# One PSUM bank per head for the first scores of an attention decoder

## The reference

```
# windowed cross attention to the context, 16 heads of 16 features, |i - j| <= 64
scores = where(local, q @ k.T / 4, -inf);  p = softmax(scores);  ctx = p @ v
# cell of six nodes, each an attention of 8 heads of 32 features
q = ew0 * (n_q @ We_q + b);  k = ...;  v = ...
o = softmax((q Wq)(k Wk).T / sqrt(32)) @ (v Wv) @ Wo;   node = act_w * o + q
# cross attention of layer 1, 16 heads of 16 features, padded keys masked
p = softmax(where(mask, ln(q) @ ln(k).T / 4, -inf));  ctx = p @ v
```

## Time and profile before

| | us |
|---|---|
| median of three runs | 3567.08 (3566.13 to 3568.82) |
| the profiled execution | 3568.07 |
| its span in the trace | 3566.3 |
| PE busy | 3242.3 (91% of the span) |
| DVE busy | 2329.9 (65%) |
| ACT busy | 1695.1 (48%) |
| POOL busy | 1019.1 (29%) |

### The profile page before, as it was taken

One profiled execution on the slowest core, in us unless ns is written; L12 is line 12 of the kernel. 1 busy time (PEld: TensorE's weight loads), 2 busy tenths in 40 slices (PEclk: granted clock), 3 DMA queues, 4 the chain that ended last, 5 costly groups with the idle time before them and its releaser, 6 DMA issues.

```text
span 3566.3 us, 77500 instructions
## 1 busy us (share of the span) xinstructions
PE 3242.3 (91%) x31372; PEld 2395.2 (67%) x31372; DVE 2329.9 (65%) x4137; ACT 1695.1 (48%) x3472; POOL 1019.1 (29%) x795
## 2 busy tenths in 40 slices
PE   7899999998999999899999999999899999999876
PEld 6777767676766667676666766667676666766644
DVE  6675658667676766767577675766767676464533
ACT  1244454544545455444635445354454545554532
POOL 7872006042331413333041332304233141000000
PEclk8999999999999999999999999999999999999986
DMA  6210011010101101010100101101010110100000
GB/s 207 89 45 31 19 29 39 29 40 19 46 19 40 31 23 46 16 41 26 37 28 25 43 19 37 31 29 39 19 46 19 40 31 16 37 14 10 13 7 4
DMA packets 123276, 122.88 MB, mean 34 GB/s; under 512 B 9776, under 2 KB 122672, under 8 KB 122800
## 3 DMA queue, kind: packets, MB, share of 16 engines
q1 hardware_dynamic: 122928, 117.91, 10.9%
HBM read 113.69 MB, written 4.19 MB: 33 GB/s over the span
## 4 chain that ended last, share of the span: by engine, by line
PE 60%; DVE 15%; ACT 9%; issue 8%; POOL 7%; DMA 1%; SPq 0%; DVEq 0%; POOLq 0%; ACTq 0%
PE banks L747 16%; PE banks L739 11%; PE banks L892 7%; PE banks L917 6%; DVE nmx L1251 5%; PE banks L945 5%; POOL work L1641 3%; ACT work L1482 3%; PE banks L732 2%; PE banks L754 2%; PE banks L855 2%; PE banks L903 2%; POOL work L1631 2%; PE banks L952 1%; PE banks L921 1%
## 5 line engine op out<-in xcount | busy, mean ns | idle before, releaser
L747 PE MATMUL banks<-work,weights 128*128 128x256 f32 x3584 | 868.3, 390 | 56.4 <-DVE work L1275 51.5
L1251 DVE TENSOR_REDUCE nmx<-banks 128x4 f32<-128x1024 f32 (+3 forms) x684 | 725.4, 1099 | 250.5 <-PE banks L892 248.7
L747 PEld LDWEIGHTS banks<-work,weights 128*128 128x128 f32 x3584 | 678.3, 194 | 189.0 <-DVE work L1275 53.9
L1482 ACT ACTIVATE work<-banks 128x1024 f32<-128x1024 f32 (+3 forms) x679 | 595.1, 937 | 288.7 <-PE banks L921 288.7
L739 PE MATMUL banks<-weights,work 128*128 128x256 f32 x2688 | 653.7, 389 | 20.7 <-ACT work L1482 4.4
L739 PEld LDWEIGHTS banks<-weights,work 128*128 128x128 f32 x2688 | 499.3, 193 | 124.9 <-issue 39.7
L1641 POOL TENSOR_TENSOR work<-work 128x512 f32<-128x512 f32 x256 | 407.3, 1615 | 366.4 <-DVE work L1221 216.9
L892 PE MATMUL banks<-work 32*128 32x256 f32 (+1 forms) x5120 | 357.5, 394 | 60.5 <-DVE nmx L1251 27.2
L917 PE MATMUL banks<-work 32*128 32x256 f32 (+1 forms) x5120 | 391.4, 394 | 18.0 <-DVE nmx L1251 6.8
L1631 POOL TENSOR_TENSOR work<-work 128x512 f32<-128x512 f32 x256 | 346.6, 1375 | 148.7 <-DVE work L1217 134.7
L1269 DVE TENSOR_TENSOR added<-work 128x1024 f32<-128x1024 f32 x192 | 281.3, 1469 | 129.3 <-ACT work L1482 118.7
(11 more groups left out here) (156 smaller groups left out, 3525.2 us busy)
## 6 DMA issues: line engine op xcount, KB each, us to landing
weights<-in_w_all SPq DMA_DIRECT2D x322, 256.0 KB, 2.8
work<-in_w_setup SPq DMA_DIRECT2D x41, 256.0 KB, 5.1
work<-in_ctx SPq DMA_DIRECT2D x32, 256.0 KB, 3.1
work<-in_x SPq DMA_DIRECT2D x16, 256.0 KB, 3.0
out<-work SPq DMA_DIRECT2D x16, 256.0 KB, 2.2
weights<-in_w_all SPq DMA_DIRECT2D x1, 3072.0 KB, 15.0
row<-in_rows SPq DMA_DIRECT2D x1, 1280.0 KB, 9.2
mrow<-in_mask SPq DMA_DIRECT2D x16, 32.0 KB, 3.2
```

What stands on the lines that cost most here:

```text
L747: ins = e.matmul(b[:, m * 256:m * 256 + 256], wslot(w)[:, k, m * P:m * P + P], xin[:, k, :], start=(k == 0 and (m == 0 or closed)) if star ...
L1251: ins = e.tensor_reduce(nmax(s, n)[:, 2 * p + j:2 * p + end, :], b.rearrange("p j (c n) -> p j c n", c=NC)[:, :, :, 0:w], AX, ALU.max, neg ...
L1482: ins = e.activation(dst, b.rearrange("p j (c n) -> p j c n", c=NC)[:, :, :, 0:w], ACT.Exp)
```

## The change

`s` now takes four units of kind "misc", that is any four single banks, each picked as the one with the fewest free neighbours. Each head's maxima are one DVE instruction of 512 (2 x 384 for `x`) which waits for that head's products alone and gives its bank back. The plan's durations are 0.6 for each (0.47 for `x`) in place of 1.13 (0.87) for each pair. The list of seeds is another and has seven numbers instead of ten.

```diff
--- before.py
+++ after.py
@@ -70,7 +70,7 @@
 FIRST_ROWS = 3
 RSLOT = {n: i for i, n in enumerate(ROWS)}
 
-SEEDS = (981929, 264616, 376881, 660340, 622402, 125658, 701981, 998496, 712956, 113630)
+SEEDS = (703881, 34614, 376671, 349031, 315147, 108807, 15133)
 SLOTS = 10
 X, CT, XT = 0, 1, 2
 Z = 7
@@ -207,8 +207,8 @@
     def heads(n, q, k, v):
         kind, c, f, par = quad(n)
         b = do("PE", "s", n, 0.88 if kind != "x" else 1.4, q, k, *((nm_done[n - 2],) if n >= 2 else ()),
-               takes=("score", "score"))
-        maxed = [do("DVE", "s", (n, p), 1.13 if kind != "x" else 0.87, b, frees=((b, p),)) for p in range(2)]
+               takes=("misc",) * 4)
+        maxed = [do("DVE", "s", (n, g), 0.6 if kind != "x" else 0.47, b, frees=((b, g),)) for g in range(4)]
         maxed = [do("DVE", "split", n, 0.36, *maxed)]
         b = do("PE", "nm", n, 0.22, *maxed, *((st_done[n - 2],) if n >= 2 else ()), takes=("misc",))
         nm_done[n] = b
@@ -751,7 +751,7 @@
 
             def banded(b, count):
                 for j in range(count):
-                    e.matmul(b[j // 2][j % 2].rearrange("p (c n) -> p c n", c=NC)[:, :, 0:SPAN], ident_bf[:, :],
+                    e.matmul(b[j].rearrange("p (c n) -> p c n", c=NC)[:, :, 0:SPAN], ident_bf[:, :],
                              band[:, :, :], start=True, stop=False)
 
             def product(b, pairs):
@@ -883,19 +883,18 @@
                     elif kind == "c":
                         e.wait_ge(*when("cq", c, i))
                         e.wait_ge(*when("ck", c, i))
-                    b = [take("score", "max", a, 0, i), take("score", "max", a, 1, i)]
+                    b = [take("misc", "max", a, g, i) for g in range(4)]
                     if kind == "x":
                         banded(b, 4)
                     for cc in range(NC):
                         kk = queries(kind, cc)
                         for g in range(4):
-                            ins = e.matmul(b[g // 2][g % 2][:, cc * 256:cc * 256 + kk.stop - kk.start],
+                            ins = e.matmul(b[g][:, cc * 256:cc * 256 + kk.stop - kk.start],
                                            q[32 * g:32 * g + 32, f, cc * P:cc * P + P],
                                            k[32 * g:32 * g + 32, f, kk], start=(kind != "x"),
                                            stop=(kind != "x" or cc == NC - 1), tile_position=(32 * g, 0))
-                            if cc == NC - 1 and g == 1:
-                                ins.then_inc(*tell(pe[s], "s mm", a, 0, i))
-                    ins.then_inc(*tell(pe[s], "s mm", a, 1, i))
+                            if cc == NC - 1:
+                                ins.then_inc(*tell(pe[s], "s mm", a, g, i))
                 elif op == "nm":
                     e.wait_ge(*when("split", a, i))
                     b = take("misc", "nm", a, i)
@@ -908,7 +907,7 @@
                     b = [take("score", "exp", a, 0, i), take("score", "exp", a, 1, i)]
                     book(i, a)
                     if kind == "x":
-                        banded(b, 4)
+                        banded(b[0] + b[1], 4)
                     e.wait_ge(*when("nm", a, i))
                     for kc in range(NC):
                         qq = queries(kind, kc)
@@ -1247,13 +1246,11 @@
                     if n >= 2 and p == 0:
                         e.wait_ge(*when("nm mm", n - 2, i))
                     w = SPAN if kind == "x" else S
-                    for j, end, b in spans("max", n, p, i):
-                        ins = e.tensor_reduce(nmax(s, n)[:, 2 * p + j:2 * p + end, :],
-                                              b.rearrange("p j (c n) -> p j c n", c=NC)[:, :, :, 0:w], AX, ALU.max, negate=True)
-                    ins.then_inc(*freed("max", n, p, i))
+                    e.tensor_reduce(nmax(s, n)[:, p, :], at("max", n, p, i).rearrange("p (c n) -> p c n", c=NC)[:, :, 0:w],
+                                    AX, ALU.max, negate=True).then_inc(*freed("max", n, p, i))
                 elif op == "split":
-                    for p in range(2):
-                        e.wait_ge(*when("max", a, p, i))
+                    for g in range(4):
+                        e.wait_ge(*when("max", a, g, i))
                     e.tensor_tensor(nmax(s, a, 1), nmax(s, a, 0), nmax_upper(s, a, 0), ALU.subtract).then_inc(
                         *tell(vec[s], "lower bits", a, i))
                     e.wait_ge(*when("lower bits", a, i))
```

## The result

The changed kernel takes 3627.28 us (median of four runs, 3626.08 to 3628.80) against 3566.61 us before: a ratio of 1.0172, 95% interval 1.0154 to 1.019. It is slower by 61 us, where 23 us less were forecast, and outside the range.

A forecast was written before the change was run, and what follows sets the result against it. PE, 91% busy, sets the time. Interval: 191.5 + 12 + 3.2 + 2.7 = 209.4 us, 2.2 less; eleven give -24, ends +0.5, so 3544 us median; likeliest range 3515 to 3560, 8 in 10 3490 to 3606.

The forecast's parts named there:

- the plain work of PE: PE's pure work in one interval between stores: 195.7 us less 1.9 and 2.3, so 191.5 us.
- changes of array mode: PE's queue: 0.21 us each, 9 fewer in an interval, -1.9 us; -4 in the first entries, +2.5 in the last three.
- the slow clock in the interval before: PE at 1.2 GHz behind the gap at `co` 0: 2.3 us lost to the clock per interval, expected to go.
- the long gap: PE's 4.3 us wait at `co` 0 for its `norm`; with 2.3 us of slow clock, 6.6 us go per interval.
- the dense stretch: End of `s` 16 to `co` 2 of the next entry: 12 us of waits above PE's 49.2, between 9.7 and 15.1.
- a fall of the clock needs a long gap: PE through the interval: no 4 us gap before `co` 0, so granted clock 1.00 and no clock loss.
- 3.2 walked: PE waits outside that stretch: `pv` 15, `pv` 14 and `co` 5 2.5 us, `nm` 11 0.4, `r_t` 0.3.
- 2.7 for banks: PE's waits for maxima to return banks, with new waits not seen: 2.7 us per interval, between 0 and 5.5.
- The two ends: Beginning and end of the program: -4 + 2.5 + 2 = +0.5 us.
- The price of the added instructions: DVE maxima: 596 pairs split at 0.11 us, 66 us in all, 4.1 per interval, hidden where PE has other work.
- The slower one: Rival: DVE beside POOL becomes the bound; stretch 15.1 us, interval 214.8 us, 3602 us in all; chance 0.30.
- PE's waits only change places: Rival of nothing measurable: small waits remain, tight `s` to `nm` distances eat the array modes' 1.9 us; 3567 us; chance 0.12.

The follow-up runs named there:

- singles on the old order: The changed program's single-bank maxima and returns, put on the queue and banks of the kernel before: 3612.18 us, ratio 1.0129.
- the three lists above: Both kernels with one-seed lists 1, 2 and 3: pairs 3748.5, 3725.4, 3709.3 us; single banks 3745.1, 3724.7, 3698.4 us.
- halves: Kernel before, each pair's maxima done in two instructions, both banks still given back together: 3590.55 us, ratio 1.0075.
- norm first: Kernel before, `norm` 5 moved ahead of the older entry's layer norm on ACT and DVE, twelve times each: 3560.93 us, ratio 0.999.
- filled gap: Kernel before, PE makes `eq` 0 three times, twice inside the gap at `co` 0: 3567.69 us, ratio 1.0011.

## Why the prediction was wrong

**Right: what the plain work of PE is.** 191.5 us were forecast for the interval and 191.4 measured, though two errors cancel in it. PE's work at full clock fell by 0.4 us with nine changes of array mode fewer, not by 1.9, and over the program by 6 us with 102 fewer. By that a change costs 0.04 to 0.06 us, not the 0.21 that I had read from the distances of the earlier trace rows; but runs with PE's old queue have 3139 to 3145 us of such work, so no price is shown, only that 0.21 is too much. And the slow clock in the interval before was worth 3.9 us, not 2.3: I had looked at the largest gap and missed a second fall 60 us on. It stands behind waits of 1.18 and 0.63 us (timeline of PE and window, kernel before):

```profile
1711.90 0.41 PE L903 MATMUL banks<-ident,nmx 128*128 128x128 f32 x2 [1.18 <-DVE nmx L1251]
1712.94 1.33 PE L892 MATMUL banks<-work 32*128 32x256 f32 x16 [0.63 <-DVE nmx L1251]
1713.80:1717.10 3.30, 3.30 (x30) 1.30 (x26) 3.02 (x7) 1.39 (x5) 0.00 (x0) 0.50 0.00 0
```

**Right: the long gap went, and the dense stretch became as long as said.** From `s` 16 to `co` 2 12 us were forecast above PE's 49.2. It takes 60.1, which is 10.9 more, 9.0 idle, 1.6 of clock and the rest work; DVE is busy in 55.3 of it, where I had added up 54.2. A rival had put this stretch at over 14; it came out shorter than I took.

**The step that failed first: a fall of the clock needs a long gap.** I counted the falls as gone with the 4.3 us gap and expected a clock of 1.00. There are three in nine of the eleven intervals, after waits of 2.1, 2.1, and 0.95 with 1.05. That is 4.9 us in each of these where none were counted and 49 us over the eleven, and it alone turns the forecast. It is 49 of the 62 us by which the eleven intervals together missed it. Against the kernel before, which lost 45 us there, it is little more: the loss that was to go stayed. The run in which one such wait was filled confirms it for the changed kernel: 11 us. At 2.1 us of idle time the forecast of no fall was not worked out from any row; the earlier trace rows showed a fall at 4.3 and I took that for the size that it needs, while the trace had the one at 1713 too. The same wait of 2.14 us doesn't always bring a fall. At 1868.16, shown above, it does; two intervals further on it doesn't (timeline of PE, and the windows behind both):

```profile
1868.16:1872.50 4.34, 4.34 (x48) 2.33 (x52) 3.06 (x5) 1.29 (x4) 0.00 (x0) 0.61 0.00 0
...
2297.51 1.15 PE L892 MATMUL banks<-work 32*128 32x256 f32 x16 [2.14 <-ACT work L1479]
2297.54:2301.88 4.34, 4.34 (x67) 2.69 (x68) 3.73 (x7) 2.10 (x7) 0.41 (x1) 1.00 0.00 0
```

There are 22 such waits in the eleven intervals, and 20 have a fall beside them.

**The second: waits outside the stretch.** 5.9 us were forecast (3.2 walked, 2.7 for banks) and some 10 measured. The sum was saved by the stretch, where 9.0 us of idle time stand for the 12 forecast; but all three falls follow waits for ACT that I didn't have. 7.2 us of the new waits outside the stretch end with ACT. I had walked PE's and DVE's queues and costed ACT at nothing because it is half idle. The wait at 1781 shows how that fails (timeline of DVE, of the DMA queue and of ACT):

```profile
1773.82 1.92 DVE L1200 TENSOR_SCALAR work<-work,mv,rstd 128x256 f32<-128x256 f32 x2
...
1776.26 0.41 SPq L1732 DMA_DIRECT2D work<-in_x  x1
...
1779.11 0.76 DVE L1177 BATCH_NORM_STATS2 st<-work 128x6 f32<-128x256 f32 x2 [0.45 <-DMA work<-in_x]
...
1780.18 0.30 ACT L1387 ACTIVATE lnv<-mv,eps 128x2 f32<-128x2 f32 x1 [2.89 <-DVE mv L1181]
1780.51 0.20 ACT L1390 ACTIVATE rstd<-lnv 128x2 f32<-128x2 f32 x1
1780.62 0.82 ACT L1381 ACTIVATE work<-banks,nb 128x256 f32<-128x256 f32 x2
```

ACT itself is idle for 2.9 us, since the head of its queue is the root of a layer norm that isn't ready. It is the first layer norm of a new entry. Its data are loaded only when the last layer norm (L1200) of the entry that had the place before is done, at the end of the dense stretch; the load is issued at 1776.26 and has landed at 1779.1, where DVE itself waits for it. Behind the root stands `co` 2's eviction (L1381), which PE waits for. DVE's lateness doesn't end at `co` 2, where my walk ended; it goes on through a load and through another engine's queue.

**The third: the ends.** The two ends were to cost 0.5 us together. The first two entries cost 8 and the last three 15 (7 of idle time, 8 of clock). With singles on the old order the last three cost 7, so order has its part in it.

**The price of the added instructions** was not a term of its own in the forecast: I called it hidden outside the stretch and the tail. On a fixed order it is 24 us of time for 37 us more DVE work. In the changed kernel it can't be separated, for the order is another. Single banks on the old order lose 46 us (in the profiled executions 24 of clock, 15 of idle time and 4 of work), and the changed order 15 more. So three quarters of the loss are there without any new order. Of that my forecast knew nothing, and its rivals neither: I had tied the change's fate to the order. The old order is one that suits pairs, though, and the three lists above show no such loss.

**The rivals.** The slower one had the interval nearly right (214.8 for 215.1) and named DVE beside POOL in the stretch. That mechanism isn't what happened: the split's mean is 278 ns in the changed kernel,

```profile
L1257 DVE TENSOR_TENSOR nmx<-nmx 128x8 f32<-128x8 f32 x320 | 89.1, 278 | 11.1 <-DVE nmx L1254 0.2
```

below the 349 of the earlier trace rows, and the stretch is shorter than its price. Its 2.3 us for a slow clock behind one wait was the right kind of term, two times too small. The rule that it cited from the Trainium skill (SBUF — State Buffer, Who interferes with whom), that a split and a POOL product lock each other out, stays in accord with the earlier trace rows, but decided nothing. "PE's waits only change places" was said of small ones; it is true of the largest. Priced at 6.6 us in an interval, the gap brought 4 us in the whole program when it was taken away alone.

**What stays open.** Why single returns make the clock fall four times in an interval and pair returns mostly twice, on one order and with the same idle time and the same waits, isn't settled; a test would be a kernel whose waits come a little earlier or later but are as long. Nor is how much of the changed kernel's 61 us its list could still win: with five lists single banks ranged from 3627 to 3745, and no list was looked for here.

## What to carry to other kernels

A gap on the busiest engine is worth its length only if the next instruction behind it isn't held by the same late queue. Before pricing it, look who the two or three steps behind it wait for. Read every fall of the granted clock off the trace before, not only the one at the largest gap. Where a half idle engine has an in-order queue, ask what stands at its head, not how busy it is. And where a list of seeds sets the order, compare a change on a fixed order or on several lists: a single list here was worth up to 235 us, ten times the 24 that the added instructions cost.

## What the runs showed of the hardware

- The granted clock of PE fell to 0.50 behind single waits of 2.1 us and behind two of 1 us close together, in a stream of products that was otherwise dense. Each fall cost some 1.7 us of work. With one order in one run, intervals of 208.7 and 213.7 us came out by it.
- No length of a wait decided alone whether the clock fell: beside waits of 2.14 us in 20 of 22 cases (changed kernel), beside waits of 2.07 us in eight and four of eleven (singles and halves), beside waits of 3.25 us in seven of eleven (norm first).
- PE time that is saved can be lost again to the clock: with the gap filled or removed, the clock fell at a place some 20 us further on (filled gap), or beside the wait that had moved (norm first).
- Two single banks' maxima one behind the other took 1.29 us, a pair 1.18; but the 596 splits raised DVE's busy time by only 37 us on the fixed order, 0.06 each.
